# Decay attention: the scores of a head pair in two row halves of the array, and the decay logarithms brought to all partitions by transfers

## The chip, the core and the metric

The kernel runs on one core of a Trainium2 chip. The metric is the device time of one execution in microseconds (us); lower is better. The time of the kernel before is the median of three runs.

## What is computed

The program is a stack of four residual layers over x with shape (2, 1024, 128): differential attention, a mixture of experts, decay attention, a mixture of experts. The change lies in the third, whose reference is, in short:

```
q = elu(x @ Wq) + 1;  k = elu(x @ Wk) + 1;  v = x @ Wv        # 16 heads of 64
a = sigmoid(x @ Wa + ba + 2.0)                                # one decay per token and head
S[t] = a[t] * S[t-1] + k[t] v[t]^T;   z[t] = a[t] * z[t-1] + k[t]
out[t] = (q[t] S[t]) / (q[t] z[t] + 1e-6);   y = out @ Wo
```

The kernel computes it in chunks of 128 tokens. Let L be the running sum of log a within a chunk. Inside the chunk, the weight of key m for query n is exp(L[n] - L[m]) times q[n].k[m], for m up to n. What came before the chunk enters through the carried state S, scaled by exp(L[n]). All of it is fp32.

## The kernel before

`decay_attention` (L1221) works on 16 chunks, which the code calls steps t = 0 to 15, each of 128 tokens and 16 heads. The heads are taken in four groups of four (i = 0 to 3, "slots") or in eight pairs (hp). Before the steps, `layer_norm` (L46) normalises x and turns it (XNT). In it POOL runs `constants()` (L1292 to L1311) and TensorE the decay logits (L1316). Then comes a prologue: log a is formed, summed by a matmul (L1494), copied to L (L1805), negated to nL (L1810), and the first chunk's projections are made.

There is no scheduler. The order of each engine's work is written out by hand in its `step` function (L1466 for TensorE, L1572 for ACT, L1670 for POOL, L1769 for VectorE), and semaphores tie the engines together. All queues are in order. One step of TensorE (PE in the profile), with the lines, is:

- slot 0; the second half of the last chunk's state product (`state`, L1449); `keys` of the next chunk (L1334, WK)
- slot 1; `state`, first half; then twice `values` (L1334, WV) and `outputs_turn` (L1383, turns the last chunk's outputs YN)
- slot 2; then twice `keys_turn` (L1371, turns the next chunk's keys Kn into the bank TR) and `queries` (L1355)
- slot 3; `project_out` of the last chunk (L1390)

A slot i is four blocks: `decays` (L1398) for the next group, `across_chunks` (L1424, q times the carried state, into OX), `within_chunk` (L1432, weights WB times V1, into OI), `scores` (L1412) of the next group into AT.

The decay weights of a group are made like this. `decays` multiplies a selector `pick` (bf16, one row of ones per head) with LT, which holds L turned and split into three bf16 parts, so that the bank LB holds L[n] of a head on all 128 partitions. ACT (`exp_decay`, L1569) forms exp(LB - L[m]) into DM, four instructions of 128x128, one per head. POOL cuts the upper triangle off (`mask`: a one-column gate L1639 and the select L1641). VectorE (`weigh`, L1731) multiplies AT by DM into WB. DM and WB have two buffers, LB and AT one bank each. So `decays` of a group waits for `exp_decay` of the group before, and `exp_decay` waits for `weigh` of two groups before.

The scores of a head contract over 64 values. Keys are turned in pairs, 64 rows for the one head and 64 for the other. ACT (`kt_copy`, L1551) copies each half to its own place in KTZ, whose other half is zero (memset once, L1311). So each head's scores are a matmul over all 128 rows, half of them zero.

ACT also does, for the projections, Relu and Exp of `exp_` (L1532, L1534), `v_copy` (L1542) and `yt_copy` (L1558). VectorE does elu (L1709), `combine` (L1738, L1742: OI plus scaled OX), `reciprocals` (L1749, L1751), `update` of the state (L1759) and `add_out` (L1767). POOL does `divide` (L1667), `keys_decayed` (L1648) and `state_decayed` (L1658).

Two waits matter for what follows. The second `keys_turn` shares the bank TR with the first and waits for its `kt_copy`. And VectorE runs, at the end of a step, this order:

```
elu_queries(n, nb)      # waits for ACT's Exp of the query projections
combine(t, b, 3)
reciprocals(t, b)
weigh(n, 0)             # the next step's within_chunk waits for it
```

## Time and profile before

| | us |
|---|---|
| three runs, median (lowest, highest) | 1275.2 (1273.15, 1275.52) |
| the profiled execution, device time | 1278.41 |
| its span in the profile | 1276.6 |
| TensorE matmul busy over the span | 1068.2 (84%) |
| VectorE, ACT, POOL busy | 762.1 (60%), 744.3 (58%), 451.8 (35%) |

The profile is of one execution. Times in its rows count from the start of the span. The decay attention lies from 723.7 us, where its layer norm begins, to about 1108 us, where its last output is added. A row of the timeline gives the start, the length from the first start to the last end of a merged group, engine, line, operation, output <- inputs, shape, count, and in brackets how long the engine sat idle before it and what ended the wait. Matmuls overlap in the array, so the cost of a block of matmuls is read from its start to the next block's start, not from its length. An fp32 matmul is recorded as two, so four heads show as x8.

### The profile page before, as it was taken

What the parts mean: (1) busy time and instruction counts of PE and PEld (TensorE: products, weight loads), DVE (VectorE), ACT (ScalarE), POOL (GpSimd) and SP (SyncE); (2) the same over time, 40 slices, a digit from 0 to 9 for tenths busy, and PEclk for the clock granted to TensorE, in tenths of its full rate; (3) what the DMA queues carried; (4) which work ended last, traced back from release to release, by engine and by line L of the source; (5) the groups of instructions that cost most, each with busy time, mean ns of one, the idle gap of its engine ahead of it and who ended that gap; (6) DMA issues with size and microseconds to landing.
All of it is one profiled execution on the core that took longest, in us unless ns stands there. A gap on an engine that the chain in (4) does not pass through costs nothing. (4 is left out here: it accounts for less than half of the span.)

```text
span 1276.6 us, 26889 instructions
## 1 busy us (share of the span) xinstructions
PE 1068.2 (84%) x10226; PEld 756.0 (59%) x10226; DVE 762.1 (60%) x1517; ACT 744.3 (58%) x1493; POOL 451.8 (35%) x597
## 2 busy tenths in 40 slices
PE   5269999999999886666999179999999999669994
PEld 3113333333333334565999157888888888559994
DVE  6288898988888825964333635454545454463333
ACT  5207888888787882122566265656565666216663
POOL 5202112112212213423675414343434343316762
PEclk9659999999999997755999679999999999859997
DMA  3511011011101006022111200000000000011123
GB/s 92 188 52 27 27 28 51 27 28 49 29 27 35 19 2 202 1 60 62 49 49 39 74 1 2 1 1 2 2 1 2 1 2 2 9 33 47 48 47 114
DMA packets 37821, 48.85 MB, mean 38 GB/s; under 512 B 9728, under 2 KB 20480, under 8 KB 37696
## 3 DMA queue, kind: packets, MB, share of 16 engines
q1 hardware_dynamic: 31552, 34.81, 9.2%
q0 software_dynamic: 4992, 10.23, 2.9%
q8 instruction: 84, 1.38, 0.4%
q10 hardware_dynamic: 1152, 2.10, 0.4%
q14 instruction: 41, 0.34, 0.1%
HBM read 32.13 MB, written 14.55 MB: 37 GB/s over the span
## 5 line engine op out<-in xcount | busy, mean ns | idle before, releaser
L551 ACT ACTIVATE PB<-S 128x512 f32<-128x512 f32 x576 | 310.2, 598 | 121.5 <-PE S L474 118.3
L592 DVE TENSOR_REDUCE mx<-S 128x2 f32<-128x1024 f32 (+1 forms) x192 | 207.4, 1129 | 21.0 <-PE S L460 20.9
L566 POOL TENSOR_SCALAR_AFFINE_SELECT PB<-PB 128x512 f32<-128x512 f32 x128 | 78.9, 634 | 364.1 <-ACT PB L551 364.1
L507 PE MATMUL PV<-PB,VP 128*32 128x256 f32 (+2 forms) x2560 | 182.0, 371 | 18.0 <-ACT OT L541 17.0
L1193 DVE TENSOR_TENSOR m_hs<-m_gs,m_UP 128x512 f32<-128x512 f32 x78 | 53.7, 688 | 158.6 <-ACT m_gs L1053 156.5
L460 PE MATMUL S<-W 48*128 48x512 bf16 (+3 forms) x640 | 97.6, 338 | 36.5 <-DVE mx L571 22.1
L474 PE MATMUL S<-W 50*128 50x512 bf16 (+3 forms) x768 | 122.2, 329 | 1.0
L507 PEld LDWEIGHTS PV<-PB,VP 128*32 128x32 f32 x2560 | 54.1, 109 | 87.4 <-issue 55.6
L914 POOL DMA_INDIRECT m_xs<-xn_rows,m_source x78 | 75.4, 967 | 81.3 <-DVE m_source L1168 58.1
L460 PEld LDWEIGHTS S<-W 48*128 48x128 bf16 x640 | 27.2, 96 | 127.4 <-issue 46.8
L1059 ACT ACTIVATE m_wgu<-W 128x1024 f32 x78 | 82.5, 1058 | 30.3 <-DVE m_etab L1173 28.9
L920 POOL DMA_INDIRECT yd_rows<-m_ys,m_target x78 | 76.7, 983 | 61.9 <-DVE m_ys L1200 61.9
L582 DVE TENSOR_REDUCE mx<-S 128x8 f32<-128x1024 f32 x64 | 78.3, 1224 | 21.5 <-PE S L453 20.8
L1569 ACT ACTIVATE d_DM<-d_LB,d_nlc 128x128 f32<-128x128 f32 x256 | 72.4, 367 | 25.1 <-PE d_LB L1398 24.5
L1000 PE MATMUL m_GP<-m_xt,m_wgu 128*128 128x128 f32 x624 | 85.3, 281 | 1.9 <-ACT m_xt L1049 1.8
L1009 PE MATMUL m_YP<-W,m_hs 128*128 x624 | 82.8, 276 | 1.8 <-DVE m_ys L1200 1.2
L1000 PE MATMUL m_UP<-m_xt,m_wgu 128*128 128x128 f32 x624 | 84.1, 279 | 0.0
L1000 PEld LDWEIGHTS m_GP<-m_xt,m_wgu 128*128 128x128 f32 x624 | 78.2, 197 | 3.4 <-issue 3.4
L1639 POOL TENSOR_TENSOR d_gate<-ident 128x1 f32<-128x1 f32 x64 | 12.4, 193 | 189.1 <-ACT d_DM L1569 189.1
L1000 PEld LDWEIGHTS m_UP<-m_xt,m_wgu 128*128 128x128 f32 x624 | 77.7, 196 | 0.0
L1009 PEld LDWEIGHTS m_YP<-W,m_hs 128*128 128x128 f32 x624 | 75.8, 192 | 2.5 <-issue 2.5
L1412 PE MATMUL d_AT<-d_QT,d_KTZ 128*128 128x128 f32 x512 | 72.5, 286 | 0.0
(260 smaller groups left out, 2072.0 us busy)
## 6 DMA issues: line engine op xcount, KB each, us to landing
W<-qk_parts SPq DMA_DIRECT2D x224, 32.0 KB
qk_parts<-OT SPq DMA_DIRECT2D x24, 256.0 KB
W<-qk_parts SPq DMA_DIRECT2D x32, 96.0 KB
W<-qk_parts SPq DMA_DIRECT2D x32, 64.0 KB
W<-in_L_ffn_w_gate SPq DMA_DIRECT2D x1, 2048.0 KB, 10.8
W<-in_L_ffn_w_up SPq DMA_DIRECT2D x1, 2048.0 KB, 15.7
xn_rows<-m_XN SPq DMA_DIRECT2D x8, 256.0 KB, 2.3
m_GB<-yd_rows SPq DMA_DIRECT2D x8, 256.0 KB, 5.5
```

Of the source, the lines that this page charges most:

```text
L460: ins = nc.tensor.matmul(S1[:, b, a, 256 * k:256 * k + w], QS[base:base + KR, s, h, qb * P:(qb + 1) * P], KS[base:base + KR, s, h, c * 512 ...
L474: ins = nc.tensor.matmul(S2[:, j % 3, col:end], KS[base:base + KM, s, h, kb * P:(kb + 1) * P], QS[base:base + KM, s, h, q0:q0 + end - col] ...
L507: ins = nc.tensor.matmul(PV[32 * u:32 * u + 32, shift + col:shift + end], VP[:, g, kb, u // 2, :], PB[:, slot, col:end], start=(kb == 0 an ...
L551: nc.scalar.activation(PB[:, j % NPB, :], S2[:, j % 3, :], ACT.Exp, scale=SC).then_inc(exp_done, 1)
L566: nc.gpsimd.affine_select(out=tri, in_=tri, compare_op=ALU.is_ge, fill=0.0, base=0, pattern=[[0, U], [1, P]], channel_multiplier=-1).then_ ...
L582: nc.vector.reduce_max(mx[:, g % 2, 2].rearrange("p a h q -> p (a h) q")[:, :, q:q + 2], S1[:, b].rearrange("p a (h j k) -> p (a h) j k", ...
L592: nc.vector.reduce_max(mx[:, g % 2, c, :, heads[0], qb], S1[:, b, :, 0:w], AX.X)\
L914: pool.indirect_dma_start(out=xs[:, s % XB], out_offset=None, in_=XD[:, :], in_offset=bass.IndirectOffsetOnAxis(ap=source[:, s:s + 1], axi ...
L920: pool.indirect_dma_start(out=YD[:, :], out_offset=bass.IndirectOffsetOnAxis(ap=target[:, s:s + 1], axis=0), in_=ys[:, s % YB], in_offset= ...
L1000: last = nc.tensor.matmul(H[:, s % 2, j * P:(j + 1) * P], wgu[:, s % 2, k, j * P:(j + 1) * P], xt[:, s % 2], start=True, stop=True)
L1009: last = nc.tensor.matmul(YP[:, 0:P], hs[:, s % 2, j * P:(j + 1) * P], WD[:, bass.ds(e, 1), j, :].rearrange("p o d -> p (o d)"), start=(j ...
L1059: nc.scalar.activation(wgu[:, s % 2], W3[:, 0:2 * n].rearrange("p (k e f) -> p k e f", k=2, e=E) [:, :, bass.ds(e, 1), :].rearrange("p k o ...
```

## The change

What it does, part by part:

- **Decays.** `decays`, the bank LB, `pick`, LT and the three bf16 parts are gone. Instead TensorE turns L once (two transposes, in the prologue), VectorE copies the result (LTS), and SyncE stores it to a DRAM tensor (`LR`, 128 KB). For every step SyncE then loads row t of it (16 heads of 128 values, 8 KB) to all 128 partitions: LQ, 1 MB per step, two buffers. The load for t is issued once `exp_decay` of step t - 2 is all done. `exp_decay` reads LQ from SBUF. Its bias is nL itself, so the copy nlc (L1633, L1691) is gone.
- **DM** has four buffers, one per group. `exp_decay(t, i)` waits for `weigh(t - 1, i)` only, and for the load at i = 0.
- **Scores.** Keys stay where the transpose puts them (KT): `kt_copy` is one ACT instruction of 128x512 for two of 64x512. The scores of a head are a matmul over 64 rows, the even head in rows 0 to 63 and the odd one in rows 64 to 127. The two write to two different banks (AT is now two banks), and they alternate in the order. DM and WB are laid out to match.
- **Buffers.** enegs has two buffers for four, with a wait for ACT's own Exp two before. Some prologue tensors share memory with O.
- **Constants on POOL.** In `constants()` these go: the zeroing of `pick1`, its three selects and the cast to `pick` (L1295, L1303, L1307), the memsets of LT (L1308) and KTZ (L1311). The memset of V1 shrinks from all 128x2080 elements to the column of ones, 128x32.

The diff, cut to its core:

```
...
-        LT = sb("LT", [P, NT, P], BF16)
-        pick = sb("pick", [P, H, P], BF16)
-        pick1 = sb("pick1", [P, H])
+        LTS = sb("LTS", [P, 2, P])
+        LQ = sb("LQ", [P, 2, H, P])
...
-        zz, mz, ez, lz = (sb(n, [P, NT, H]) for n in ("zz", "mz", "ez", "lz"))
-        Lp = sb("Lp", [P, NT, 3, H], BF16)
-        Lr = sb("Lr", [P, NT, H])
...
-        nlc = sb("nlc", [P, 2, H])
...
-        enegs = sb("enegs", [P, 4, 512])
+        enegs = sb("enegs", [P, 2, 512])
...
-        KTZ = sb("KTZ", [P, 2, HP, 2, P])
+        KT = sb("KT", [P, 2, HP, P])
...
-        DM = sb("DM", [P, 2, 4, P])
-        WB = sb("WB", [P, 2, 4, P])
+        DM = sb("DM", [P, 4, 2, 2, P])
+        WB = sb("WB", [P, 2, 2, 2, P])
...
+        zz, mz, ez, lz, rem = (O[:].rearrange("p b h v -> p (b h v)")[:, m * NT * H:(m + 1) * NT * H]
+                               .rearrange("p (t h) -> p t h", h=H) for m in range(5))
         rd = sb("rd", [P, H])
...
-        PA, AT, LB = psum("PA", [P, 2, 512]), psum("AT", [P, 4, P]), psum("LB", [P, 4, P])
+        PA, AT = psum("PA", [P, 2, 512]), psum("AT", [P, 2, 512])
...
+        ZP, LP, TP, LTP = AT[:, 0], OI, OX, SU
...
+            nc.gpsimd.memset(V1[:, :, :, DH:VW], 1.0).then_inc(const_d, 1)
...
-            nc.gpsimd.memset(V1[:], 1.0).then_inc(const_d, 1)
-            nc.gpsimd.memset(KTZ[:], 0.0).then_inc(const_d, 1)
...
+            @block.sync
+            def _(sp):
+                sp.wait_ge(lt_copied, 1)
+                sp.dma_start(LR.rearrange("(g t) h n -> (t h) g n", g=2), LTS[:]).then_inc(lt_stored, 16)
+                sp.wait_ge(lt_stored, 16)
+                for t in range(NT):
+                    if t >= 2:
+                        sp.wait_ge(expd_done, (t - 1) * 4)
+                    sp.dma_start(LQ[:, t % 2].rearrange("p h n -> p (h n)"),
+                                 LR[t].rearrange("h n -> (h n)").partition_broadcast(P)).then_inc(lq_loaded[t % 2], 16)
...
-                def decays(t, b, i):
-                    if i or from_(t, 1):
-                        pe.wait_ge(expd_done, t * 4 + i)
-                    for j in range(4):
-                        last = nc.tensor.matmul(LB[:, j], pick[:, 4 * i + j],
-                                                LT[:, bass.ds(t, 1), :].rearrange("p o n -> p (o n)"),
-                                                start=True, stop=True)
-                    last.then_inc(lb_done, 1)
...
-                    for j in range(4):
-                        h = 4 * i + j
-                        last = nc.tensor.matmul(AT[:, j], KTZ[:, b, h // 2, h % 2, :], QT[:, b, h // 2, :],
-                                                start=True, stop=True)
+                    for r in range(2):
+                        for a in range(2):
+                            q = slice(64 * a, 64 * a + 64)
+                            last = nc.tensor.matmul(AT[:, a, r * P:(r + 1) * P], KT[q, b, 2 * i + r], QT[q, b, 2 * i + r],
+                                                    start=True, stop=True)
...
-                    if i < 3:
-                        decays(t, b, i + 1)
-                    elif not last:
-                        decays(t + 1, 1 - b, 0)
...
+                pe.wait_ge(l_ready, 1)
+                for g in range(2):
+                    last = nc.tensor.transpose(LTP[:, g * P:(g + 1) * P],
+                                               L[:, 8 * g:8 * g + 8].rearrange("p t h -> p (t h)"), ident[:])
+                last.then_inc(lt_done, 1)
...
+                    if n * 4 + k >= 2:
+                        act.wait_ge(exp_done, n * 4 + k - 1)
+                    nc.scalar.activation(enegs[:, k % 2], PA[:, j % 2], ACT.Relu, scale=-1.0).then_inc(neg_done, 1)
...
-                    for h in range(2):
-                        q = slice(64 * h, 64 * h + 64)
-                        last = nc.scalar.activation(KTZ[q, b, 4 * c:4 * c + 4, h, :], TR[q], ACT.Copy)
-                    last.then_inc(kt_copied, 1)
+                    nc.scalar.activation(KT[:, b, 4 * c:4 * c + 4], TR[:], ACT.Copy).then_inc(kt_copied, 1)
...
-                    act.wait_ge(lb_done, t * 4 + (i + 1))
                     if i == 0:
-                        act.wait_ge(xc_ready, t + 1)
-                    if i >= 2 or from_(t, 1):
-                        act.wait_ge(w_done, t * 4 + (i - 1))
+                        act.wait_ge(lq_loaded[b], 16 * (t // 2 + 1))
+                    if from_(t, 1):
+                        act.wait_ge(w_done, (t - 1) * 4 + (i + 1))
                     for j in range(4):
                         h = 4 * i + j
-                        last = nc.scalar.activation(DM[:, i % 2, j], LB[:, j], ACT.Exp, bias=nlc[:, b, h:h + 1])
+                        last = nc.scalar.activation(DM[:, i, j % 2, j // 2], LQ[:, b, h], ACT.Exp, bias=nL[:, t, h:h + 1])
                     last.then_inc(expd_done, 1)
                 def step(t, b, last=False):
...
-                        pool.wait_ge(expd_done, (n - 1) * 4)
-                    nc.gpsimd.tensor_copy(xc[:, b], XNT[:, bass.ds(n * P, P)])
-                    nc.gpsimd.tensor_copy(nlc[:, b], nL[:, bass.ds(n, 1), :].rearrange("p o h -> p (o h)"))\
-                      .then_inc(xc_ready, 1)
+                    nc.gpsimd.tensor_copy(xc[:, b], XNT[:, bass.ds(n * P, P)]).then_inc(xc_ready, 1)
...
-                    nc.vector.tensor_tensor(WB[:, i % 2], AT[:], DM[:, i % 2], ALU.mult).then_inc(w_done, 1)
+                    nc.vector.tensor_tensor(WB[:, i % 2].rearrange("p a r n -> p a (r n)"), AT[:, :, 0:2 * P],
+                                            DM[:, i].rearrange("p a r n -> p a (r n)"), ALU.mult).then_inc(w_done, 1)
...
+                dve.wait_ge(lt_done, 1)
+                nc.vector.tensor_copy(LTS[:].rearrange("p g n -> p (g n)"), LTP[:, 0:2 * P]).then_inc(lt_copied, 1)
...
-                chain.link(nc.vector.tensor_copy(Lp[:, :, 0], L[:]))
-                chain.link(nc.vector.tensor_tensor(Lr[:], L[:], Lp[:, :, 0], ALU.subtract))
-                chain.link(nc.vector.tensor_copy(Lp[:, :, 1], Lr[:]))
-                nc.vector.tensor_tensor(Lp[:, :, 2], Lr[:], Lp[:, :, 1], ALU.subtract).then_inc(lp_ready, 1)
...
```

TensorE in one step, before, from `queries` in slot 2 to `scores` in slot 0 of the next step (d_LB is the decays' bank, d_AT the scores', d_OX and d_OI the outputs'):

```order
L1355 MATMUL d_PA<-d_xc,d_WQ 128x128 x4
L1398 MATMUL d_LB<-d_LT,d_pick 128x128 x4
L1424 MATMUL d_OX<-d_S,d_QT 128x130 x2
L1432 MATMUL d_OI<-d_V,d_WB 128x65 x4
L1412 MATMUL d_AT<-d_QT,d_KTZ 128x128 x4
L1390 MATMUL d_SU<-d_WO,d_YTS 128x128 x8
L1398 MATMUL d_LB<-d_LT,d_pick 128x128 x4
L1424 MATMUL d_OX<-d_S,d_QT 128x130 x2
L1432 MATMUL d_OI<-d_V,d_WB 128x65 x4
L1412 MATMUL d_AT<-d_QT,d_KTZ 128x128 x4
```

The same stretch now:

```order
L1353 MATMUL d_PA<-d_xc,d_WQ 128x128 x4
L1414 MATMUL d_OX<-d_S,d_QT 128x130 x2
L1422 MATMUL d_OI<-d_V,d_WB 128x65 x4
L1402 MATMUL d_AT<-d_QT,d_KT 128x128 x4
L1388 MATMUL d_SU<-d_WO,d_YTS 128x128 x8
L1414 MATMUL d_OX<-d_S,d_QT 128x130 x2
L1422 MATMUL d_OI<-d_V,d_WB 128x65 x4
L1402 MATMUL d_AT<-d_QT,d_KT 128x128 x4
```

The four decay matmuls of each slot are gone; nothing else changed its place.

ACT from the first `kt_copy` of a step to the Relu and Exp of the next keys, now (d_KT is the turned keys, d_enegs and d_etmp are Relu's and Exp's outputs):

```order
L1530 ACTIVATE d_KT<-d_TR 128x512
L1513 ACTIVATE d_enegs<-d_PA 128x512
L1515 ACTIVATE d_etmp<-d_enegs 128x512
L1530 ACTIVATE d_KT<-d_TR 128x512
L1513 ACTIVATE d_enegs<-d_PA 128x512
L1515 ACTIVATE d_etmp<-d_enegs 128x512
L1546 ACTIVATE d_DM<-d_LQ,d_nL 128x128 x8
```

Before, the copies L1530 were two instructions each (L1551), and the rest stood in the same order. The eight exponentials at the end are those of group 0 and of group 1 of the next step; the second four no longer wait for TensorE in between.

## Rows read from the trace of the kernel before

**Rows 1.** Windows: stretch, its length, PE, PEld, DVE, ACT, POOL busy, PEclk, DMA, GB/s.

```profile
800.00:1060.00 260.00, 254.92 (x2254) 219.97 (x2253) 133.59 (x280) 165.87 (x393) 113.48 (x173) 1.00 0.01 1
```

**Rows 2.** Timeline of PE, from the turned keys of one step to those of the next.

```profile
907.38 0.60 PE L1371 MATMUL d_TR<-ident,d_Kn 128*128 128x128 f32 x4
907.82 1.06 PE L1355 MATMUL d_PA<-d_xc,d_WQ 128*128 128x128 f32 x8
909.27 0.66 PE L1371 MATMUL d_TR<-ident,d_Kn 128*128 128x128 f32 x4 [0.39 <-ACT d_KTZ L1551]
...
910.66 0.39 PE L1398 MATMUL d_LB<-d_LT,d_pick 128*128 128x128 bf16 x4
910.88 0.67 PE L1424 MATMUL d_OX<-d_S,d_QT 128*128 128x130 f32 x4
911.38 1.00 PE L1432 MATMUL d_OI<-d_V,d_WB 128*128 128x65 f32 x8
912.22 1.11 PE L1412 MATMUL d_AT<-d_QT,d_KTZ 128*128 128x128 f32 x8
913.17 1.95 PE L1390 MATMUL d_SU<-d_WO,d_YTS 128*128 128x128 f32 x16
...
915.68 1.09 PE L1432 MATMUL d_OI<-d_V,d_WB 128*128 128x65 f32 x8
916.61 1.11 PE L1412 MATMUL d_AT<-d_QT,d_KTZ 128*128 128x128 f32 x8
917.65 0.69 PE L1449 MATMUL d_SU<-d_V,d_KS 128*64 128x65 f32 x16
...
928.61 0.27 PE L1371 MATMUL d_TR<-ident,d_Kn 128*128 128x128 f32 x1
```

**Rows 3.** Timeline of ACT, the first part of the same step.

```profile
908.02 1.20 ACT L1551 ACTIVATE d_KTZ<-d_TR 64x512 f32<-64x512 f32 x2 [1.32 <-PE d_TR L1371]
909.24 0.60 ACT L1532 ACTIVATE d_enegs<-d_PA 128x512 f32<-128x512 f32 x1
...
910.40 1.18 ACT L1551 ACTIVATE d_KTZ<-d_TR 64x512 f32<-64x512 f32 x2
911.61 0.60 ACT L1532 ACTIVATE d_enegs<-d_PA 128x512 f32<-128x512 f32 x1
...
912.77 1.12 ACT L1569 ACTIVATE d_DM<-d_LB,d_nlc 128x128 f32<-128x128 f32 x4
```

**Rows 4.** Timeline of DVE and POOL in that part.

```profile
912.90 0.69 DVE L1709 SCALAR_TENSOR_TENSOR d_QT<-d_PA,d_etmp 128x512 f32<-128x512 f32 x1 [1.61 <-ACT d_etmp L1534]
...
914.11 0.64 POOL L1641 TENSOR_SCALAR_AFFINE_SELECT d_DM<-d_DM 128x512 f32<-128x512 f32 x1
```

**Rows 5.** Timeline of PE in the differential attention, row halves in bf16.

```profile
304.54 0.39 PE L453 MATMUL S<-W 48*128 48x128 bf16 x8
```

**Rows 6.** Timeline of POOL and DVE in the layer norm of the decay attention.

```profile
731.06 3.50 POOL L1311 MEMSET d_KTZ<- 128x4096 f32 x1
...
728.13 6.46 DVE L89 TENSOR_SCALAR d_ln_ve<-d_ln_mv 128x16 f32<-128x16 f32 x1
```

**Rows 7.** The instructions of line L89: shortest, median and longest in ns, first and last start.

```profile
L89 DVE TENSOR_SCALAR lna_ve<-lna_mv x1: 174/174/174, 10.9 to 10.9; 128x16 f32<-128x16 f32 x1
```

**Rows 8.** Timeline of DVE, ACT and PE in the prologue.

```profile
751.49 0.42 DVE L1805 COPY d_L<-d_OI 128x256 f32<-128x256 f32 x1 [1.31 <-PE d_OX L1495]
...
764.40 1.14 ACT L1569 ACTIVATE d_DM<-d_LB,d_nlc 128x128 f32<-128x128 f32 x4 [0.58 <-issue]
...
767.32 1.11 PE L1432 MATMUL d_OI<-d_V,d_WB 128*128 128x65 f32 x8
```

**Rows 9.** DMA issues on the page: out<-in, queue, count, KB each, us from issue to landing.

```profile
W<-in_L_ffn_w_gate SPq DMA_DIRECT2D x1, 2048.0 KB, 10.8
...
xn_rows<-m_XN SPq DMA_DIRECT2D x8, 256.0 KB, 2.3
m_GB<-yd_rows SPq DMA_DIRECT2D x8, 256.0 KB, 5.5
```

More of the change, by code:

```diff
@@ L1294, in constants @@
             nc.gpsimd.memset(triu[:], 1.0).then_inc(const_d, 1)
-            nc.gpsimd.memset(pick1[:], 0.0).then_inc(const_d, 1)
-            nc.gpsimd.wait_ge(const_d, 3)
+            nc.gpsimd.wait_ge(const_d, 2)
             nc.gpsimd.affine_select(out=triu[:], in_=triu[:], compare_op=ALU.is_ge, fill=0.0, base=0,
                                     pattern=[[1, P]], channel_multiplier=-1).then_inc(const_d, 1)
-            for part in range(3):
-                if part:
-                    nc.gpsimd.wait_ge(const_d, 4 + part)
-                nc.gpsimd.affine_select(out=pick1[:], in_=pick1[:], compare_op=ALU.not_equal, fill=1.0,
-                                        base=-H * part, pattern=[[-1, H]],
-                                        channel_multiplier=1).then_inc(const_d, 1)
-            nc.gpsimd.wait_ge(const_d, 7)
-            nc.gpsimd.tensor_copy(pick[:], pick1[:].unsqueeze(2).to_broadcast([P, H, P])).then_inc(const_d, 1)
-            nc.gpsimd.memset(LT[:].bitcast(U32), 0).then_inc(const_d, 1)
+            nc.gpsimd.memset(V1[:, :, :, DH:VW], 1.0).then_inc(const_d, 1)
             nc.gpsimd.memset(S[:], 0.0).then_inc(const_d, 1)
-            nc.gpsimd.memset(V1[:], 1.0).then_inc(const_d, 1)
-            nc.gpsimd.memset(KTZ[:], 0.0).then_inc(const_d, 1)
         def decay_logits(t):
@@ L1431, in within_chunk @@
                         h = 4 * i + j
-                        last = nc.tensor.matmul(OI[:, j * VW:(j + 1) * VW], WB[:, i % 2, j, :], V1[:, b, h, :],
+                        last = nc.tensor.matmul(OI[:, j * VW:(j + 1) * VW], WB[:, i % 2, j % 2, j // 2], V1[:, b, h, :],
                                                 start=True, stop=True)
@@ L1500, in _ @@
                     queries(0, 0, c)
-                pe.wait_ge(lp_ready, 1)
-                for q in range(NT // 4):
-                    if q >= 2:
-                        pe.wait_ge(lt_copied, q - 1)
-                    for j in range(4):
-                        last = nc.tensor.matmul(LTP[q % 2][:, j * P:(j + 1) * P],
-                                                Lp[:, 4 * q + j].rearrange("p a h -> p (a h)"), identb[:],
-                                                start=True, stop=True)
-                    last.then_inc(lt_done, 1)
-                pe.wait_ge(lt_copied, NT // 4)
-                decays(0, 0, 0)
                 scores(0, 0, 0)
@@ L1531, in exp_ @@
                         act.wait_ge(elu_done, n * 4 + (k - 3))
-                    nc.scalar.activation(enegs[:, k], PA[:, j % 2], ACT.Relu, scale=-1.0).then_inc(neg_done, 1)
+                    if n * 4 + k >= 2:
+                        act.wait_ge(exp_done, n * 4 + k - 1)
+                    nc.scalar.activation(enegs[:, k % 2], PA[:, j % 2], ACT.Relu, scale=-1.0).then_inc(neg_done, 1)
                     act.wait_ge(neg_done, n * 4 + (k + 1))
-                    nc.scalar.activation(etmp[:, k], enegs[:, k], ACT.Exp, scale=-1.0).then_inc(exp_done, 1)
+                    nc.scalar.activation(etmp[:, k], enegs[:, k % 2], ACT.Exp, scale=-1.0).then_inc(exp_done, 1)
                 def v_copy(n, b, c):
@@ L1610, in _ @@
                     exp_(0, 2 + c, 4 + c)
-                for q in range(NT // 4):
-                    act.wait_ge(lt_done, q + 1)
-                    nc.scalar.activation(LT[0:3 * H, 4 * q:4 * q + 4].rearrange("p t n -> p (t n)"), LTP[q % 2], ACT.Copy)\
-                      .then_inc(lt_copied, 1)
-                act.wait_ge(nlc_ready, 2)
+                act.wait_ge(nl_ready, 1)
                 exp_decay(0, 0, 0)
@@ L1688, in _ @@
                     nc.gpsimd.tensor_copy(xc[:, n], XNT[:, n * P:(n + 1) * P]).then_inc(xc_ready, 1)
-                pool.wait_ge(nl_ready, 1)
-                for n in range(2):
-                    nc.gpsimd.tensor_copy(nlc[:, n], nL[:, n, :]).then_inc(nlc_ready, 1)
                 pool.wait_ge(cut_ready, 4)
```

25 lines of the change are left out of this document (13 added, 12 removed).

## The prediction

> **What bounds the kernel now.** I read the windows first, over the steady steps of the decay attention. TensorE is busy 254.92 of 260 us there, at the full granted clock, while VectorE has 133.59, ACT 165.87 and POOL 113.48 [rows 1]. So in this stage time is TensorE's, and each block taken from it counts until another engine's chain comes late. The timeline of TensorE then gives the step: from the turned keys of one step to those of the next it is 907.38 to 928.61, 21.23 us [rows 2]. I cut it at the first `within_chunk` (915.68) into part A, 8.30 us, and part B, 12.93 us. The timelines of ACT, VectorE and POOL show what runs beside part A [rows 3, 4].
>
> The last view is the timeline of the layer norm ahead of the stage. One VectorE instruction on 16 columns took 6.46 us there and ended at 734.59 (728.13 + 6.46), 0.03 after POOL's memset of KTZ (731.06 + 3.50) [rows 6]. The same line in the first layer norm took 0.174 us [rows 7]. Everything in the stage waits for it.
>
> **Constants.** POOL's long memsets and the cast go. What is left of them is memsets of 128, 128, 32 and 1040 columns and a select: at KTZ's rate (4096 columns in 3.50) under 2 us from the start at 723.7, well before VectorE's 728.13. I take the stall as gone: 6.46 - 0.17 = **6.3 us**. Lower bound 0, if POOL isn't its cause.
>
> **Decays.** Four bf16 matmuls cost 910.66 to 910.88, 0.22 us per slot [rows 2]. The block behind them, `across_chunks`, costs 0.50 for four records of 130 columns. Its fp32 records are 0.11 apart, so about 0.05 of it is the change of type, and it goes too: 0.27 per slot, 1.09 per step.
>
> **Scores.** A full block is 912.22 to 913.17, 0.95, and 1.04 where the column-tiled state product follows (916.61 to 917.65) [rows 2]. The difference, 0.09, is the price of one change of tiling. No row shows fp32 matmuls in row halves. Near rows: in bf16, eight records in row halves took 0.39 from first start to last end [rows 5], as long as four records over all rows (0.39) [rows 2], so the halves ran side by side. In fp32, 16 records of 65 columns in column halves took 0.69, less a tail of 0.16 some 0.035 each, under a third of the 0.112 of a whole record of 128 columns; half the size alone would give a half. (0.112 is 1.79 over 16 in `project_out`, part A below.) I take four pairs at the fp32 pitch of 0.112: 0.45, plus 0.09 to change in and 0.09 to change out, 0.63. That saves 0.32 in the slots 2 and 3, and 0.41 in the slots 0 and 1, where the change out was paid already. The other end is no overlap: 0.95 + 0.18 = 1.13, a loss of 0.09 or 0.18 per slot.
>
> The Trainium skill (TensorEngine Tiling (Array Packing), Key Properties) says that changing the tiling mode drains the engine. By a full drain each change would cost about 0.17, since a matmul of the transposes ends 0.17 after the next one could start (0.60 against 0.44 in rows 2); the row says 0.09. With 0.17 at four changes in part B the step would be 0.3 longer, 5 us in all.
>
> **Key copy.** One ACT instruction of 128x512 from PSUM takes 0.60 (`exp_`, L1532) [rows 3], against 1.20 for the two halves. TensorE's second `keys_turn` sat 909.27 - 907.82 - 0.89 = 0.56 us behind it. (Queries cost 910.66 - 909.27 = 1.39 less 0.44 for the turn and 0.06 for its late start.)
>
> **Part A now.** TensorE: turn 0.44, queries 0.89 (1.33). The copy starts 0.64 after the turn began (908.02), ends at 1.24, and no longer holds the second turn. Turn and queries again: 2.66. `across_chunks` 0.45, `within_chunk` 0.84 (911.38 to 912.22), scores 0.63, `project_out` 1.79 (913.17 to 915.68 less 0.22 and 0.50), `across_chunks` 0.45: **6.82**. Beside it runs the chain of ACT and VectorE. Query Relu from 1.33 + 0.17 + 0.04 = 1.54; the second key copy 1.16 later as before (909.24 to 910.40), 2.70; the next Relu behind it at 3.27; elu 1.29 later (911.61 to 912.90), 4.56. From this elu over `combine`, `reciprocals` and `weigh` to `within_chunk` it was 915.68 - 912.90 = 2.78: **7.34**. The mask is in time: exponential to mask's end was 914.75 - 912.77 = 1.98, now 3.27 + 1.16 (911.61 to 912.77) + 1.98 = 6.41, and `weigh`, 0.7 long, starts about 6.6. So the chain ends last, TensorE waits 0.5, and part A falls from 8.30 to 7.34: **0.96**. Half of what TensorE gives up there is swallowed.
>
> **Part B now.** Two decays with their 0.05 (0.54), the second and third `across_chunks` among them, and three score blocks (0.41 + 0.41 + 0.32 = 1.14): 12.93 - 1.68 = 11.25. I checked who could be late. Key Relus come right behind the matmuls as before, `weigh` of group 1 and 3 needs only AT, since ACT makes their exponentials early, and mask 2 follows ACT by 1.98 more than a microsecond ahead of its use. I take no new wait: **1.68**.
>
> So a step is 18.6 instead of 21.2: 2.64 saved, 14 times from the first turn to the last, 37.0. The first step has part B without the state product (1.5); the last has part A and three slots, and its end hangs on `combine` (2.3). Steps together: **40.8**.
>
> **New work.** SyncE loads 1 MB per step. Rows near it: 2048 KB landed in 10.8, so 5.4 for half; 256 KB landed in 5.5, four of those in a row would be 22 [rows 9]. I take 6.5, by the large one. It has more than a step: issued when the last exponentials of t - 2 are done (near the start of part A), needed 18.6 + 4.4 = 23 us later. Hidden, and other DMA in this stage is about 1 GB/s [rows 1]. ACT's exponentials read SBUF now; they are off the chain by that 0.2 us, and I leave them at 1.12 for four.
>
> The Trainium skill (DMA: Bandwidth & Descriptors, Anatomy of one DMA) gives a fit of 2.0 us plus bytes over 436 GB/s. By it 1 MB is an estimated 4.4 us, and the sum below would be 2 us smaller, by the first load.
>
> **Prologue.** L is copied from 751.49 and the first exponential ran at 764.40, the first `within_chunk` at 767.32 [rows 8]. Now VectorE waits for two transposes and copies them (about 753.1), the store takes 2.3 [rows 9], the load 6.5: 762. The projections' own chain, held up 1.2 by VectorE's new wait but rid of four copies of LT and two half copies, ends about there too. Exponential at 762.5 or so, less 764.40, and some way for the first scores: I take **1.5** saved; between 4 saved and, with a slow load, 13 lost.
>
> **Sum.** 6.3 + 40.8 + 1.5 = 48.6 us. On the profiled execution's 1278.4 that is 1229.8; the median of the runs is 3.2 below this execution, and I forecast a median of **1227**.
>
> **Rivals.**
>
> *Row halves of fp32 do not overlap.* For it: no row shows them in fp32, and loading 128 fp32 weight columns may be what sets the 0.112. Against it: column halves in fp32 do overlap [rows 2]. Each score block is then 1.13. Part B: 12.93 - 0.54 + 0.36 = 12.75; part A: TensorE 7.32, still the chain's 7.34. A step 20.1, saved 1.14, 16 over 14 steps and 2 at the ends: 18 + 7.8 = 26, **1249**. Chance 0.13.
>
> *The chain of ACT and VectorE keeps part A at its length.* For it: VectorE and ACT are strictly in order, and eight exponentials now stand in a row behind the query chain; POOL may also hold VectorE's small instruction of `reciprocals`, as it held L89. Then only part B and the ends gain: 1.68 x 14 + 3 = 26.5, plus 7.8: 34, **1241**. Chance 0.10.
>
> *The transfers become the bound.* 128 partitions read the same 8 KB of DRAM, which no row shows. It decides once a load takes over 21.2 us, as four 256 KB transfers in a row would (22). A step is then 22.3 or so, 1.1 x 14 = 15 lost; the first load comes 16 later than I take, so 13 lost in the prologue instead of 1.5 saved; the constants still give 6.3: 22 lost, **1297**. Against it: the large load's 190 GB/s. Chance 0.04.
>
> *The stall is not POOL's.* Its end 0.03 after the memset's speaks against that. 42 saved, **1233**, chance 0.03, inside the range.
>
> **How the numbers follow.** The forecast, with steps between 18.3 and 19.2 us, has 0.70: 1219 to 1236. The range goes on to the first rival's 1249 and stops at **1217 to 1250**: outside are the slow transfers, the worse half of the first rival, and about 0.07 beyond the forecast's ends. A measurement of this kernel can tell 0.2%, 2.6 us. Faster 0.94, within 0.2% 0.01 (for a load just about at the bound), slower 0.05 (the slow transfers, and 0.01 for what I don't see).
>
> **What the next profile would show.** Right: line L89 in the decay's layer norm under 0.5 us; eight records of d_AT about 0.45 to 0.5 from first start to last start, in pairs that start together; a step of 18.6 between two turns of the keys; a wait of about 0.5 before the first d_OI of a step, by VectorE; none behind the key copy; loads of LQ landing in under 10 us. Wrong: pairs of d_AT 0.112 apart one by one (1249), exponentials waiting for a transfer (1297), or a wait of TensorE before the d_OI of slots 1 to 3, which I set to none.

## The result and the profile after

| | before | after |
|---|---|---|
| runs, median (lowest, highest), us | 1274.18 (1272.26, 1275.52) | 1238.84 (1236.01, 1243.42) |
| profiled execution, device time | 1278.41 | 1240.70 |
| its span | 1276.6 | 1238.9 |

The ratio is 0.9727, 95% interval 0.9691 to 0.9763: faster, by 35.3 us in the medians. 48.6 had been predicted. The direction is right and the time lies in the range of 1217 to 1250, but a quarter of the gain is missing, and 1238.84 is outside the band of 1219 to 1236 that had the chance of 0.70. It is nearer the 1241 of the second rival (the chain keeps part A at its length), whose mechanism the rows below don't show. Both medians are of four runs.

I divide the difference of the two spans by place first. "Turn 0" is the first turned keys of the first step, "turn 14" those of the fifteenth.

| stretch | before | after | difference | predicted |
|---|---|---|---|---|
| up to the decay's layer norm | 723.70 | 722.71 | -1.0 | 0 |
| layer norm | 22.61 | 16.64 | -6.0 | -6.3 |
| prologue, to the first `within_chunk` | 21.01 | 19.77 | -1.2 | -1.5 |
| from there to turn 0 | 11.16 | 13.03 | +1.9 | -1.5 |
| turn 0 to turn 14 | 298.70 | 268.98 | -29.7 | -37.0 |
| turn 14 to the last add | 31.02 | 28.68 | -2.3 | -2.3 |
| the mixture of experts behind | 168.40 | 169.07 | +0.7 | 0 |

So two rows fail: the fourteen steps by 7.3 us, and the first step by 3.4. The rest is as it was laid out; the first row is no effect of the change, since that layer norm starts between 719.3 and 725.1 in the profiles of the changed kernel and its variants. The windows of the steady stage, in the columns of [rows 1], are still full of TensorE:

```profile
800.00:1040.00 240.00, 237.88 (x2122) 195.65 (x2120) 139.37 (x293) 158.68 (x377) 116.89 (x165) 1.00 0.15 54
```

TensorE is busy 99% of it at the full granted clock, as before. The transfers show as a DMA share of 0.15. The timeline of TensorE over one step, to hold against [rows 2]:

```profile
889.13 0.66 PE L1369 MATMUL d_TR<-ident,d_Kn 128*128 128x128 f32 x4
889.62 1.06 PE L1353 MATMUL d_PA<-d_xc,d_WQ 128*128 128x128 f32 x8
890.51 0.61 PE L1369 MATMUL d_TR<-ident,d_Kn 128*128 128x128 f32 x4
...
891.86 0.61 PE L1414 MATMUL d_OX<-d_S,d_QT 128*128 128x130 f32 x4
892.31 1.00 PE L1422 MATMUL d_OI<-d_V,d_WB 128*128 128x65 f32 x8
893.24 0.72 PE L1402 MATMUL d_AT<-d_QT,d_KT 64*128 64x128 f32 x8
893.88 2.05 PE L1388 MATMUL d_SU<-d_WO,d_YTS 128*128 128x128 f32 x16
895.77 0.61 PE L1414 MATMUL d_OX<-d_S,d_QT 128*128 128x130 f32 x4
896.55 1.11 PE L1422 MATMUL d_OI<-d_V,d_WB 128*128 128x65 f32 x8 [0.17 <-DVE d_WB L1699]
897.59 0.71 PE L1402 MATMUL d_AT<-d_QT,d_KT 64*128 64x128 f32 x8
898.24 0.69 PE L1439 MATMUL d_SU<-d_V,d_KS 128*64 128x65 f32 x16
...
908.13 0.66 PE L1369 MATMUL d_TR<-ident,d_Kn 128*128 128x128 f32 x4
```

The step is 908.13 - 889.13 = 19.00 us (before 21.23, predicted 18.6). From the turn to the first `within_chunk` (part A) it is 896.55 - 889.13 = 7.42, where 7.34 was predicted. The wait there is 0.33: `across_chunks` sits 896.55 - 895.77 = 0.78 ahead of it instead of 0.45. The bracket says 0.17, since the modelled end of the matmuls covers the rest. It is VectorE's, as the prediction had it. The second turn waits for nothing. Part B is 908.13 - 896.55 = 11.58, where 11.25 was predicted. It has no wait either, so what is missing there is in the length of its blocks.

In `scores` (L1402) the eight records come as four pairs, 6 to 7 ns apart within a pair, and the pairs follow at the 0.11 of a single full record. So fp32 row halves do overlap. But the block is 0.65 from its start to the next one's, not 0.45 with a 0.09 behind it, and the `within_chunk` ahead of it takes 892.31 to 893.24, 0.93, where 0.84 is plain. The single records of the block at 897.59 give the pairs at 897.59, 897.80, 897.92 and 898.03, and the next block at 898.24: 0.21, 0.11, 0.11, 0.21. The first pair stands 0.10 too long. The weight loads show the same: that of the second pair starts at 897.70, 0.11 after the first pair's matmuls, where those of the third and fourth start with the matmuls of the pair ahead of them. Changing in costs 0.09 ahead of the block, changing out 0.09, and **inside the block the second pair comes 0.10 late**. That is the term that the sum lacks. Where full rows follow, their second matmul is late too: `project_out` 895.77 - 893.88 = 1.89 for 1.79, the turn 0.49 for 0.44.

The Trainium skill (TensorEngine Tiling (Array Packing), Key Properties) says that changing the mode drains the engine. That fits the 0.09 on each side; the 0.10 behind the first pair is on top.

The same part on ACT, VectorE and POOL:

```profile
889.82 0.60 ACT L1530 ACTIVATE d_KT<-d_TR 128x512 f32<-128x512 f32 x1 [0.76 <-PE d_TR L1369]
...
893.52 2.43 ACT L1546 ACTIVATE d_DM<-d_LQ,d_nL 128x128 f32<-128x128 f32 x8
...
893.64 0.69 DVE L1677 SCALAR_TENSOR_TENSOR d_QT<-d_PA,d_etmp 128x512 f32<-128x512 f32 x1 [0.87 <-ACT d_etmp L1515]
894.25 0.42 DVE L1707 TENSOR_TENSOR d_ox<-d_OX,d_eL 128x260 f32<-128x260 f32 x1
894.70 0.43 DVE L1711 TENSOR_TENSOR d_O<-d_OI,d_ox 128x260 f32<-128x260 f32 x1
895.16 0.50 DVE L1718 TENSOR_SCALAR d_rd<-d_O 128x16 f32<-128x16 f32 x1
895.70 0.25 DVE L1720 RECIPROCAL d_rd<-d_rd 128x16 f32<-128x16 f32 x1
895.87 0.63 DVE L1699 TENSOR_TENSOR d_WB<-d_AT,d_DM 128x512 f32<-128x512 f32 x1
...
895.00 0.64 POOL L1610 TENSOR_SCALAR_AFFINE_SELECT d_DM<-d_DM 128x512 f32<-128x512 f32 x1
```

The chain is that of the prediction: elu 4.51 after the turn (4.56 predicted), `combine`, the denominators, `weigh`. One instruction in it, L1718 on 16 columns, takes 0.50 and ends at 895.66, with POOL's mask at 895.64. Before it took 0.35 (914.42 to 914.77), and it ended with POOL's mask there too (914.75, [rows 4]); the shortest of the 16 took 0.174 in either kernel. Its 0.15 more accounts for the 0.13 by which this chain, from elu to `within_chunk`, is longer (2.91 for 2.78). The same kind of instruction takes 0.175 in the layer norm now, against 6.46 [rows 6]. The loads land in 4.6 us in the median:

```profile
L89 DVE TENSOR_SCALAR d_ln_ve<-d_ln_mv x1: 175/175/175, 727.1 to 727.1; 128x16 f32<-128x16 f32 x1
```

```profile
d_LQ<-l_rows SPq DMA_DIRECT2D x16, 1024.0 KB, 4.6
```

That leaves the first step. The timeline of TensorE in the prologue and ahead of the second `within_chunk` of slot 0, after:

```profile
756.17 0.71 PE L1414 MATMUL d_OX<-d_S,d_QT 128*128 128x130 f32 x4
759.12 1.97 PE L1422 MATMUL d_OI<-d_V,d_WB 128*128 128x65 f32 x8 [2.24 <-DVE d_WB L1699]
761.02 1.23 PE L1402 MATMUL d_AT<-d_QT,d_KT 64*128 64x128 f32 x8
762.18 3.65 PE L1332 MATMUL d_PA<-d_WK,d_xc 128*128 128x512 f32 x4
...
778.21 0.71 PE L1414 MATMUL d_OX<-d_S,d_QT 128*128 128x130 f32 x4 [1.23 <-DVE d_O L1711]
779.58 1.97 PE L1422 MATMUL d_OI<-d_V,d_WB 128*128 128x65 f32 x8 [0.65 <-DVE d_WB L1699]
```

TensorE waits 2.24 us there. It isn't for the transfers: the first two loads were issued at 748.6 and 748.9 and landed after 4.5 and 6.7 us, before 756, and ACT went from the Exp of the queries to the first exponential (756.23) without a gap. From that exponential over mask and `weigh` to `within_chunk` it is 2.89 us; before it was 2.92 (764.40 to 767.32, [rows 8]), but then decays, full-row scores and `across_chunks`, at half clock, kept TensorE busy in that time.

The blocks behind the wait take about twice their later length (3.65 for the key projection). The granted clock says why, in the windows of 35 us from 4 us ahead of the first `within_chunk`, after and then before:

```profile
755.00:790.00 35.00, 30.38 (x215) 23.31 (x215) 16.44 (x32) 18.88 (x47) 13.28 (x21) 0.80 0.09 31
```

```profile
763.00:798.00 35.00, 32.70 (x252) 26.61 (x249) 16.69 (x33) 19.83 (x50) 14.26 (x22) 0.90 0.01 1
```

0.80 for 0.90: the clock stands at half, 1.2 GHz for 2.4, in two stretches of 6.8 us. The first (758.7 to 765.6) begins in the wait of 2.24 us, the second (779.2 to 786.1) in the wait of 0.65 us, behind one of 1.23. Before, there were two stretches of 3.4. The four runs of the changed kernel order themselves the same way: the two shorter ones (1236.01 and 1236.97 us) have a mean granted clock of 0.906 and 0.903, the two longer ones (1240.70 and 1243.42) of 0.896 and 0.894.

**Theories.** (1) The change of tiling costs 0.28 per scores block, not 0.18; a kernel with half as many blocks gains it back. (2) The first step is lost by the clock, which fell because TensorE sat waiting before its first `within_chunk`. (3) VectorE's wait in part A is POOL's mask holding L1718. Rivals: the transfers or the reads of SBUF disturb the other engines; the order of the two halves in the program decides how well they overlap; the layer norm was shortened by something else than POOL.

### The profile page after: what moved, and what is told of

Same layout as the page of the kernel before. It is cut to its first block and busy times, and to the rows that moved or that the text cites. A ratio compares the mean times of both kernels' runs of the same rounds, so it can differ in the third digit from the quotient of the medians.

```text
span 1238.9 us, 26242 instructions
## 1 busy us (share of the span) xinstructions
PE 1039.2 (84%) x9956; PEld 719.3 (58%) x9956; DVE 755.4 (61%) x1514; ACT 728.7 (59%) x1457; POOL 442.1 (36%) x574
## 5 line engine op out<-in xcount | busy, mean ns | idle before, releaser
L1546 ACT ACTIVATE d_DM<-d_LQ,d_nL 128x128 f32<-128x128 f32 x256 | 79.3, 388 | 0.0
L1513 ACT ACTIVATE d_enegs<-d_PA 128x512 f32<-128x512 f32 x64 | 37.8, 591 | 70.0 <-PE d_PA L1332 65.6
L1422 PE MATMUL d_OI<-d_V,d_WB 128*128 128x65 f32 x512 | 67.6, 276 | 5.6 <-DVE d_WB L1699 5.6
```

The costliest lines, as they stand in the source:

```text
L1546: last = nc.scalar.activation(DM[:, i, j % 2, j // 2], LQ[:, b, h], ACT.Exp, bias=nL[:, t, h:h + 1])
```

## The experiments

All edits are to the changed kernel. A median is given with its ratio to the kernel before in the same runs.

### Which part of the change gave what

`full_rows` takes the row halves and the single key copy back and keeps the decays by transfer. KTZ is zeroed by POOL behind the layer norm.

```diff
-    q = slice(64 * a, 64 * a + 64)
-    last = nc.tensor.matmul(AT[:, a, r * P:(r + 1) * P], KT[q, b, 2 * i + r], QT[q, b, 2 * i + r],
+    last = nc.tensor.matmul(AT[:, a, r * P:(r + 1) * P], KTZ[:, b, 2 * i + r, a, :], QT[:, b, 2 * i + r],
...
-    nc.scalar.activation(KT[:, b, 4 * c:4 * c + 4], TR[:], ACT.Copy).then_inc(kt_copied, 1)
+    for h in range(2):
+        q = slice(64 * h, 64 * h + 64)
+        last = nc.scalar.activation(KTZ[q, b, 4 * c:4 * c + 4, h, :], TR[q], ACT.Copy)
+    last.then_inc(kt_copied, 1)
```

> The changed kernel with the scores over all 128 rows again (KTZ with its zero halves and two key copies), the decays still by transfers. Theory (the row halves and the single key copy carry most of the gain in a step, by about 0.75 us on TensorE in part B and about 1 us on the chain of ACT and VectorE in part A): step about 20.7 instead of 19.0, time about 1263. Rival (the decays' matmuls were what counted, and the row halves give back in changes of tiling what they save): step 19.0 to 19.5, time under 1247.

Measured: 1265.59 us, ratio 0.993 (0.9914 to 0.9947), step 20.81. Its TensorE:

```profile
898.88 0.60 PE L1370 MATMUL d_TR<-ident,d_Kn 128*128 128x128 f32 x4
...
900.77 0.66 PE L1370 MATMUL d_TR<-ident,d_Kn 128*128 128x128 f32 x4 [0.39 <-ACT d_KTZ L1534]
...
907.31 1.11 PE L1422 MATMUL d_OI<-d_V,d_WB 128*128 128x65 f32 x8 [0.52 <-DVE d_WB L1706]
```

The wait behind the key copy is back, and its part B is 20.81 - 8.43 = 12.38: 12.93 less 0.55, where 0.54 was the term for the two decays. In part A (907.31 - 898.88 = 8.43, for 8.30) the two decays give nothing, since `within_chunk` waits for VectorE. So the decays alone bring 0.42 per step, and the row halves with the single copy, put on top of that, the other 1.81. The two were not separated from each other.

### Do the transfers disturb anything?

```diff
-    for t in range(NT):
-        if t >= 2:
-            sp.wait_ge(expd_done, (t - 1) * 4)
+    for t in range(2):
...
-    act.wait_ge(lq_loaded[b], 16 * (t // 2 + 1))
+    act.wait_ge(lq_loaded[b], 16)
```

The decays of all later steps are those of the first two, and 14 MB of loads are left out.

> The changed kernel with only the first two of the 16 loads of LQ (later chunks use wrong decays, so this leaves out 14 MB of transfers). Theory (the loads are hidden and disturb nobody): step 19.0, the exponentials 388 ns as now. Rival (the loads' writes slow ACT or TensorE): the exponentials fall to 367 ns, and the step falls by 0.1 us or more.

Measured: 1241.88 us in its one run, step 19.00. The exponentials in the groups of instructions (busy, mean ns of one) before, after and with two loads:

```profile
L1569 ACT ACTIVATE d_DM<-d_LB,d_nlc 128x128 f32<-128x128 f32 x195 | 55.1, 367 | 17.8 <-PE d_LB L1398 17.8
```

```profile
L1546 ACT ACTIVATE d_DM<-d_LQ,d_nL 128x128 f32<-128x128 f32 x201 | 62.5, 387 | 0.0
```

```profile
L1544 ACT ACTIVATE d_DM<-d_LQ,d_nL 128x128 f32<-128x128 f32 x204 | 63.3, 388 | 0.0
```

The loads cost the steps nothing. The exponentials are 20 ns longer than the 367 that they took before, but without the loads as well, so it isn't contention by them. What changed is that they read LQ in SBUF instead of LB in PSUM, and nL instead of its copy as the bias; no run separates the two.

### Half as many changes of tiling

Scores of two groups stand in one block; there are two such blocks per step for four.

```diff
+    for g in range(2):
+        for r in range(2):
+            for a in range(2):
+                q = slice(64 * a, 64 * a + 64)
+                hp = 2 * (i + g) + r
+                last = nc.tensor.matmul(AT[:, a, (2 * g + r) * P:(2 * g + r + 1) * P], KT[q, b, hp],
+                                        QT[q, b, hp], start=True, stop=True)
+    last.then_inc(at_done, 2)
...
-    if i < 3:
-        scores(t, b, i + 1)
-    elif not last:
+    if i == 1:
+        scores(t, b, 2)
+    elif i == 3 and not last:
         scores(t + 1, 1 - b, 0)
```

> The changed kernel with the scores of two groups in one block (groups 2 and 3 in slot 1, groups 0 and 1 of the next chunk in slot 3), in the unused halves of the two banks. Two blocks of row halves per step instead of four. Theory (a change of tiling costs 0.09 for the array to run dry and another 0.05 to 0.10 because the second weights are not loaded ahead): part B falls by about 1.0, part A rises by about 0.1, step about 18.1. Rival (a change costs 0.09 only): step about 18.4. Rival 2 (the second group's later scores make the weighing late): step 19 or more, with waits of TensorE on VectorE in slots 0 or 1.

Measured: 1219.14 us (1218.70 to 1220.64), ratio 0.9574 (0.9558 to 0.959), step 18.03. Its TensorE:

```profile
895.90 1.16 PE L1403 MATMUL d_AT<-d_QT,d_KT 64*128 64x128 f32 x16
896.99 2.05 PE L1388 MATMUL d_SU<-d_WO,d_YTS 128*128 128x128 f32 x16
898.88 0.61 PE L1415 MATMUL d_OX<-d_S,d_QT 128*128 128x130 f32 x4
899.33 0.89 PE L1423 MATMUL d_OI<-d_V,d_WB 128*128 128x65 f32 x7
```

Sixteen records take 1.09: eight pairs at 0.112 (0.90), and 0.19 besides, as eight records took 0.45 and 0.20. So the surplus belongs to the block, not to the pair, and theory 1 holds. By it, part B has one block of 0.09 + 1.09 = 1.18 for three of 0.74: 1.04 less, and it is 18.03 - 7.49 = 10.54 for 11.58. Part A (7.49 for 7.42) keeps its length: its scores block is 0.44 longer and fills what was VectorE's wait of 0.33, so that `within_chunk` follows `across_chunks` by the plain 0.45. (`project_out` behind the block is still 1.89 for 1.79, so the block costs 0.10 more where full rows follow.) The step is 0.97 shorter, 13.6 us in fourteen. Its first step also has the full clock, which accounts for most of the other 6.1 of the 19.7 us to the changed kernel (8.91 us from the first `within_chunk` to turn 0 for 13.03, and 18.01 for 21.98 in the next period, of which the step itself explains 2.0). This beats both kernels.

### The order of the halves

```diff
-    for r in range(2):
-        for a in range(2):
+    for a in range(2):
+        for r in range(2):
```

> The changed kernel with the four score matmuls of a group in the order even, even, odd, odd instead of even, odd, even, odd. Theory (a matmul in one row half starts beside the one in the other half only if it stands next to it in the order): the eight records start as 2 single, one pair, ... and take about 0.6 to 0.8 us from first start to last start instead of 0.44, step 19.4 to 20.4. Rival (TensorE finds the free half by itself): step 19.0.

Measured: 1239.39 us in its one run, step 19.02. Its scores:

```profile
891.69 0.72 PE L1402 MATMUL d_AT<-d_QT,d_KT 64*128 64x128 f32 x8
892.34 0.94 PE L1388 MATMUL d_SU<-d_WO,d_YTS 128*128 128x128 f32 x6
```

0.65 again, and the records stand in pairs again, 13 ns apart for 6 to 7. My idea that only neighbours in the order overlap falls: with two heads of one half issued first and the two of the other behind them, the block is as long as before. How TensorE gets there, and which heads make up a pair, these rows don't tell.

### Is the first step lost by the clock?

`filled_wait` puts ten matmuls of the identity (20 records) into TensorE's wait before the first `within_chunk`.

```diff
+    if i == 0 and not from_(t, 1):
+        pe.wait_ge(lt_copied, 1)
+        for _ in range(10):
+            nc.tensor.matmul(SU[:, 0:P], ident[:], ident[:], start=True, stop=True)
     within_chunk(t, b, i)
```

> The changed kernel with 10 matmuls of the identity (20 records, about 2.2 us, result unused) in TensorE's wait ahead of the first within_chunk of the first chunk. Theory (the granted clock fell to half there after TensorE had stood still for 2.2 us, and the first two steps of 21.3 and 22.0 us pay for it): the clock stays at full, the first steps fall to about 19, and the time by 4 to 6 us. Rival (the slow first steps come from elsewhere, as the first loads): the steps stay at 21 and 22.

Measured: 1231.92 us (1230.66 to 1233.80), ratio 0.9667 (0.9644 to 0.9691). Timeline and window:

```profile
755.23 2.39 PE L1449 MATMUL d_SU<-ident 128*128 128x128 f32 x20
757.64 1.11 PE L1422 MATMUL d_OI<-d_V,d_WB 128*128 128x65 f32 x8
```

```profile
752.00:787.00 35.00, 32.61 (x279) 26.24 (x280) 18.77 (x37) 23.64 (x57) 17.27 (x25) 1.00 0.10 41
```

With the wait filled the clock stays at 1.00. From the first `within_chunk` (757.64) to turn 0 (767.63) it is 9.99 for 13.03, and the next period 19.00 for 21.98: 6.0 us, close to the 6.9 between the medians. Theory 2 is shown for this program: what the filler filled is what cost the clock. The second stretch went with the first, though the waits of 1.23 and 0.65 us ahead of it are still there (773.69 and 775.05), so they alone don't bring it down. Work that computes nothing is worth 6 to 7 us here.

But such a wait doesn't always cost the clock. `full_rows` has a longer one at the same place, and its clock stays full from 754.3 to 781.5:

```profile
761.84 1.11 PE L1422 MATMUL d_OI<-d_V,d_WB 128*128 128x65 f32 x8 [2.65 <-DVE d_WB L1706]
```

```profile
758.00:781.50 23.50, 18.42 (x145) 15.55 (x143) 11.52 (x22) 16.25 (x40) 9.17 (x17) 1.00 0.13 46
```

The two profiles of paired scores waited 1.80 and 1.79 us there and kept it too. Why 2.24 costs the clock in one program and 2.65 doesn't in another is open.

### VectorE's small instruction in part A

`late_reciprocals` puts the denominators behind `weigh`, off the chain.

```diff
     combine(t, b, 3)
-    reciprocals(t, b)
     if not last:
         weigh(n, 0)
+    reciprocals(t, b)
```

> The changed kernel with VectorE's reciprocals behind the weighing of the next step's group 0 instead of ahead of it. Theory (in part A the chain over elu, combine, reciprocals and weighing ends last, 0.33 us behind TensorE): TensorE's wait before the first within_chunk goes, part A falls from 7.42 to about 7.1, step 18.67, time 4 to 5 us shorter. Rival (the mask on POOL or the exponentials end there as late): step 18.9 to 19.0.

Measured: 1237.71 us, ratio 0.9708 (0.9681 to 0.9734), step 18.86. VectorE and POOL:

```profile
895.19 0.69 DVE L1699 TENSOR_TENSOR d_WB<-d_AT,d_DM 128x512 f32<-128x512 f32 x1 [0.53 <-POOL d_DM L1610]
895.79 0.56 DVE L1718 TENSOR_SCALAR d_rd<-d_O 128x16 f32<-128x16 f32 x1
...
894.52 0.63 POOL L1610 TENSOR_SCALAR_AFFINE_SELECT d_DM<-d_DM 128x512 f32<-128x512 f32 x1
```

0.14 per step gained of the 0.33, 2 us in fourteen; the 1.1 us between the medians is within the spread of the runs, and the 4 to 5 expected didn't come. `weigh` now waits 0.53 for the mask, which ends at 895.15: POOL's chain lay just behind VectorE's. And L1718 takes 0.56 behind `weigh`, to 896.35, where POOL runs the mask of group 1 (895.69 to 896.32). So theory 3 holds for the instruction, but the wait isn't its alone. I had the mask in time in the prediction, and it was, by little: it ended 0.23 ahead of `weigh`.

### Does POOL hold the layer norm?

`long_memsets` adds two memsets of 4096 columns behind the constants, with a wait between them; `back_to_back` adds three without one.

```diff
+    nc.gpsimd.memset(LQ[:], 0.0).then_inc(const_d, 1)
+    nc.gpsimd.wait_ge(const_d, 6)
+    nc.gpsimd.memset(LQ[:], 1.0).then_inc(const_d, 1)
```

> The changed kernel with two more memsets of 128x4096 on POOL at the end of the layer norm's constants (they fill LQ, which the loads overwrite later). Theory (POOL's long memsets hold VectorE's small instruction of line L89): POOL is busy until about 731.4, L89 goes from 0.17 to about 4.2 us and ends with the second memset, and the time rises by about 4 us. Rival (the 6.46 us came from elsewhere): L89 stays at 0.17 and the time stays.

Measured: 1241.19 us, ratio 0.9749 (0.9722 to 0.9776). L89 had been expected to be held to the second memset's end, and wasn't. It took 0.70 and ended as POOL changed from one memset to the other. But the second memset held the instruction that came next of the same kind, the first L94, 0.34 alone:

```profile
722.72 3.51 POOL L1299 MEMSET d_LQ<- 128x4096 f32 x1
726.28 3.51 POOL L1301 MEMSET d_LQ<- 128x4096 f32 x1
...
725.56 0.70 DVE L89 TENSOR_SCALAR d_ln_ve<-d_ln_mv 128x16 f32<-128x16 f32 x1
726.83 3.05 DVE L94 TENSOR_SCALAR d_etmp<-X,d_ln_mv,d_ln_rstd 128x128 f32<-128x128 f32 x1
```

It ended at 729.88, 0.08 after the memset (729.80). So the loss came, on another line: from the layer norm's first `bn_stats` to its last L94 it is 12.39 us for 9.36 in the changed kernel, 3.0 more, and the median is 2.4 us up, which is within the spread of the runs. VectorE's reciprocal L92 (0.25, from 726.54) and its `bn_aggr` ran beside the same memsets at their usual length. The gap of the semaphore wait had let L89 in; the second form has no gap.

```diff
+    nc.gpsimd.memset(KS[:], 0.0).then_inc(const_d, 1)
+    nc.gpsimd.memset(Kn[:], 0.0).then_inc(const_d, 1)
+    nc.gpsimd.memset(LQ[:], 0.0).then_inc(const_d, 1)
```

> The changed kernel with three more memsets on POOL (2048, 2048 and 4096 columns of buffers that are overwritten later), one behind the other with no semaphore wait between. In the first form of this test there was a wait between the two memsets and L89 got in after the first. Theory (VectorE's instruction is held as long as POOL's run without a gap): POOL is busy to about 731.4 on the changed kernel's clock of time, L89 is held to there and takes about 4 us, and the time rises by about 4 us. Rival (it can get in between any two POOL instructions): L89 takes under 2 us, ending with the memset in which it arrived, and the time rises by less.

Measured: 1241.97 us, ratio 0.9739 (0.9709 to 0.9769).

```profile
724.08 1.80 POOL L1300 MEMSET d_Kn<- 128x2048 f32 x1
725.83 3.51 POOL L1301 MEMSET d_LQ<- 128x4096 f32 x1
...
725.17 4.19 DVE L89 TENSOR_SCALAR d_ln_ve<-d_ln_mv 128x16 f32<-128x16 f32 x1
```

L89 takes 4.19 and ends at 729.36, 0.02 after POOL's last memset. It started during the one memset and stayed through the whole next. The stall is POOL's, and lasts as long as POOL runs without a gap. The layer norm's stretch is 13.38 us for 9.36, 4.0 more, and the first `within_chunk`, counted from the layer norm's start, comes 3.2 later. The median rose by 3.1 us, but the runs of the changed kernel spread over 7.4 us.

### Together

`paired_late_filled` has three of these edits at once: paired scores, the late denominators, the filled wait.

> Three edits together on the changed kernel: the scores of two groups in one block, the reciprocals behind the weighing, and the 10 filler matmuls ahead of the first within_chunk. Theory: with paired scores TensorE has no wait left in a step, so the late reciprocals add nothing to the step of 18.03 us; the filler holds the clock up in every run where it would fall. Step 18.03, time 1216 to 1219. Rival (each edit gives what it gave alone): step 17.9, time 1211 to 1214.

Measured: 1220.22 us (1218.71 to 1221.77), ratio 0.9578 (0.9557 to 0.9598), step 18.03, a little above the 1216 to 1219 expected. To hold it against paired scores alone on the same chip, those ran again.

> The kernel with paired scores once more, beside the one with three edits, to compare the two on one chip. Theory: step 18.03, time 1218 to 1221, equal to the three edits within 3 us.

Measured: 1220.70 us (1219.12 to 1221.05), ratio 0.9576 (0.9556 to 0.9596). The same: nothing adds. With paired scores VectorE isn't waited for in the steps, and the first step's clock was full already:

```profile
749.00:784.00 35.00, 30.43 (x271) 24.55 (x270) 18.19 (x40) 25.32 (x63) 17.27 (x23) 1.00 0.18 70
```

That is the first of the two runs of paired scores. The combined kernel ran one stretch of its first steps at half clock, 773.0 to 776.4, in spite of its filled wait (its first period is 19.50 for 18.01). So the filler doesn't secure the clock in every program, and what does is open.

## Why the prediction was right and where it was wrong

- **Constants, 6.3.** Right: 6.0, L89 at 0.175. POOL as the cause, one rival's doubt, is shown by the 4.19 us of `back_to_back` and by the 3.05 us of L94 in `long_memsets`.
- **Decays, 0.27 per slot.** Right: part B of `full_rows` fell by 0.55, the two slots' 0.54.
- **Scores, "0.45, plus 0.09 to change in and 0.09 to change out, 0.63".** This is the term that was mis-sized. The pairs overlap at the pitch of 0.112 and both changes cost 0.09, but the pair behind a change comes 0.10 late. In part B the block cost 0.09 + 0.65 = 0.74, and three of them come to 0.33 more than the sum had: exactly what part B has too much (11.58 for 11.25). I had taken the price of a change from a block's edge in the rows before, and didn't ask what the change does to the block inside. Over fourteen steps that is 4.6 us; 0.08 more in part A makes 5.7. By a full drain of 0.17 a change, the case weighed beside it, a step would have been 18.9, near the 19.0 measured, but the sides of a block cost 0.09 each, and the rest is inside it. That 0.10 was measured once more by `paired_scores`, which has fewer blocks and loses it fewer times; that the late weight load causes it is what the rows suggest, and no run tests it.
- **Key copy.** Right: no wait behind it, and it is back in `full_rows`.
- **Part A, 7.34.** Right within 0.08: VectorE's chain ends last. TensorE waits 0.33 for it, where I had 0.5, because its own blocks are longer than I took them (scores, and `project_out` and the turn behind them). The 0.08 is the longer hold of L1718, 0.15, less 0.05 by which elu came early.
- **First step, "part B without the state product (1.5)".** Wrong, by 3.4 us, and the next period by 1.4 (3.0 over the steady step there, 1.5 before): TensorE sat 2.24 us waiting for exponential, mask and `weigh`, and the clock fell. That chain is as long as before (2.89 for 2.92); new is that nothing of TensorE's covers it. The prologue's own time was right (1.2 for 1.5). The sum held the first step at full speed and didn't ask what the wait ahead of it does to the clock. `filled_wait` gives it back, down to 9.99 from its first `within_chunk` to turn 0, where 9.66 had been predicted; the 0.33 is that of part B again.
- **Loads.** Hidden, as said; they landed in 4.6 us in the median, not 6.5, near the 4.4 estimated from the Trainium skill (DMA: Bandwidth & Descriptors), whose fit is for transfers issued by GpSimd, while SyncE issues these. The first two, issued together, took 4.5 and 6.7.
- **The rivals.** Row halves that don't overlap: out, by the pairs. The chain that keeps part A: out, though its remark on POOL and the denominators proved true (0.50 for 0.175). Slow transfers: out, by the 4.6 us and by `two_loads`. A stall that is not POOL's: out, by `back_to_back`.

The time fell into the range because the two losses together are smaller than the range is wide; the band with the chance of 0.70 was missed by them. In sum, of the 48.6: 5.7 lost in the length of the steps and 4.8 at the start, nearly all by the clock, leave 38.1, beside 37.7 between the spans. The medians differ by 35.3, since the profiled execution lies 4.2 above the median before, and 1.9 after.

## What to carry to other kernels

A block in another tiling of the array has a fixed price, 0.28 us here for pairs worth 0.112 each, and up to 0.10 more in the full-row block behind it: put as many matmuls into each such block as the banks hold. Two blocks per step for four were worth 0.97 us per step. When a change takes from TensorE the work that covered a chain of other engines, look at the granted clock behind the new wait, not at the wait alone: 2.24 us of waiting went with 6.0 us lost here, though 2.65 us in `full_rows` cost no clock. And look for a VectorE instruction far over its usual length that ends with POOL's long one, because the POOL work may be the thing to move: that gave 6.0 us here.
